# Second gather stage of a graph network: 44 of 782 row gathers replaced by one-hot products on TensorE

## The reference

```python
# layer 0: messages scaled per edge, 32 relations made of 8 basis matrices
W_rel = einsum('rb,bdf->rdf', w_comp, weight)
agg = segment_sum(h[src] * norm, etype * n_nodes + dst)
x = layernorm(x + relu(einsum('rnd,rdf->nf', agg, W_rel) + h_bias + h @ loop_weight))
# layer 1: edge features, two batch norms over all edges, mean per target node
e = (h[dst] - h[src]) @ theta_w.T + h[src] @ phi_w.T
e = relu(bn(e, bn0_g, bn0_b))
e = relu(bn(e @ fc1_w.T, bn1_g, bn1_b))
x = layernorm(x + relu(segment_sum(e, dst) / max(cnt, 1) + h))
```

## Time and profile before

| | |
|---|---|
| median of three runs | 2591.09 us |
| span of the profiled execution | 2589.5 us |
| TensorE busy in the span | 1883.2 us (73%), 10210 products |
| VectorE busy | 1326.0 us (51%) |
| ScalarE busy | 618.8 us (24%) |
| GpSimd busy | 1604.8 us (62%) |
| gathers of the second stage (L698) | 782, 943 ns each, 737.7 us busy |

### The profile page before, as it was taken

The page is one execution under the profiler, slowest core; times in us unless marked ns, Lnnn a source line. Parts: engine busy times, 40 slices in busy tenths (PEclk is TensorE's granted clock), DMA queues, the critical chain, the costliest instruction groups (busy, mean ns, idle before and its releaser), DMA issues. The chain is left out here.

```text
span 2589.5 us, 40626 instructions
## 1 busy us (share of the span) xinstructions
PE 1883.2 (73%) x10210; PEld 1458.7 (56%) x10211; DVE 1326.0 (51%) x2996; ACT 618.8 (24%) x1004; POOL 1604.8 (62%) x1759
## 2 busy tenths in 40 slices
PE   4776767677777778666666666666666899999997
PEld 3766766666666667433333333333333443999996
DVE  5444343434434435654444444444444688677776
ACT  3211111111111113311111111111111675344444
POOL 6777777777777772777777777777777100950002
PEclk9988888888888889655555555555555899999999
DMA  4222222222222222534333433343334795344442
GB/s 105 74 64 72 72 64 72 69 67 71 64 72 72 64 59 68 174 123 125 114 113 117 128 114 113 113 131 114 114 113 131 272 305 175 104 152 147 150 146 83
DMA packets 124081, 291.20 MB, mean 112 GB/s; under 512 B 34957, under 2 KB 77506, under 8 KB 106224
## 3 DMA queue, kind: packets, MB, share of 16 engines
q1 hardware_dynamic: 65856, 136.12, 16.3%
q0 software_dynamic: 50048, 102.50, 15.2%
q10 hardware_dynamic: 8112, 51.91, 5.4%
HBM read 227.22 MB, written 63.18 MB: 112 GB/s over the span
## 5 line engine op out<-in xcount | busy, mean ns | idle before, releaser
L698 POOL DMA_INDIRECT G<-btab,srcT x782 | 737.7, 943 | 282.2 <-issue 180.1
L683 POOL DMA_INDIRECT G<-in_x,srcT x782 | 744.7, 952 | 246.3 <-issue 180.1
L781 PE MATMUL PS<-BIG,G 128*128 128x192 f32 x1564 | 355.8, 380 | 261.2 <-PEq L56 259.1
L907 PE MATMUL PS<-ident,G 128*128 128x128 f32 x784 | 213.4, 428 | 353.5 <-PEq L56 353.5
L781 PEld LDWEIGHTS PS<-BIG,G 128*128 128x128 f32 x1564 | 298.0, 220 | 292.3 <-issue 291.6
L907 PEld LDWEIGHTS PS<-ident,G 128*128 128x128 f32 x784 | 140.2, 217 | 446.5 <-issue 446.5
L1039 ACT ACTIVATE BIG<-PS 128x768 f32<-128x768 f32 x196 | 158.5, 809 | 785.9 <-ACTq L56 785.9
L1474 DVE TENSOR_SCALAR ohT<-PS,node_col 80x512 bf16<-80x512 f32 x196 | 146.2, 746 | 360.6 <-DVEq L56 360.4
L792 PE MATMUL PS<-BIG 128*128 128x192 f32 (+1 forms) x1584 | 328.7, 369 | 0.5 <-PEq L56 0.5
L792 PEld LDWEIGHTS PS<-BIG 128*128 128x128 f32 x1584 | 318.3, 227 | 0.6 <-issue 0.6
L1094 ACT ACTIVATE BIG<-PS 128x512 f32<-128x512 f32 x196 | 117.0, 597 | 841.9 <-ACTq L56 841.9
(11 more groups left out here) (183 smaller groups left out, 1841.6 us busy)
## 6 DMA issues: line engine op xcount, KB each, us to landing
BIG<-spill SPq DMA_DIRECT2D x90, 1024.0 KB, 4.9
spill<-BIG ACTq DMA_DIRECT2D x49, 1024.0 KB
G<-in_x,srcT POOLq DMA_INDIRECT x782, 2.5
G<-btab,srcT POOLq DMA_INDIRECT x782
typ_i<-in_edge_type SPq DMA_DIRECT2D x97, 128.0 KB
BIG<-atab SPq DMA_DIRECT2D x196, 60.0 KB
atab<-BIG SPq DMA_DIRECT2D x12, 384.0 KB, 2.8
xn<-in_x SPq DMA_DIRECT2D x48, 64.0 KB
```

What stands on the lines that cost most here:

```text
L683: nc.gpsimd.indirect_dma_start(out=G[0:n, g % 2, t, :], out_offset=None, in_=x, in_offset=bass.IndirectOffsetOnAxis(ap=srcT[0:n, TPG * g + ...
L698: nc.gpsimd.indirect_dma_start(out=G[0:n, g % 2, t, :], out_offset=None, in_=btab[:, :], in_offset=bass.IndirectOffsetOnAxis(ap=srcT[0:n, ...
L781: mm = pe.matmul(PS[:, 2 * c + q // 2, (q % 2) * ZW:(q % 2 + 1) * ZW], G[:, h, TPC * k + q, :], soh[:, p, TPC * c + q, :, :].rearrange("p ...
L907: pe.matmul(PS[:, 2 + k, q * TILE:(q + 1) * TILE], G[:, h, TPC * k + q, :], ident[:, :], start=(q == 0), stop=False, is_transpose=True, sk ...
```

## The change

In the pairs 2 to 23 the last two tiles of the pair (256 edges) are no longer gathered. The table `btab` is put into SBUF once, as three bf16 parts that add up to the f32 value, 49 windows of 128 nodes: eight units of four windows in the space of `ACC`, which is free in this stage, the rest in `tab_more`. This is done beside the first 13 chunks (`unit_high_part`, `unit_mid_part` on ScalarE, `unit_rest_part`, `unit_low_part` on VectorE, `load_unit` on SyncE).

For a pair's 256 edges, SyncE loads two rows, 64 times the low seven bits of each source and its high bits (`load_pick`). TensorE spreads them over the partitions in one product (`spread_picks`), and ScalarE adds -64 times the partition's number (`code_picks`); the code at partition p is then equal to w exactly when the source is node p of window w. VectorE compares the code with each w (`pick_hots`), which gives a one-hot matrix of 128 x 256 in bf16 for each window; code and result are single rows of 256 (`PICK_ROW, PICK_COLS, PICK_STEP = 1, 256, 256`). TensorE multiplies each window's three parts by it (`pick_rows_of`) and adds the 147 products up in PSUM bank 4. The 49 windows are done in seven batches of seven: one each beside chunks 1 to 5 of the pair, two beside chunk 6 (`picked_batches`), with room for two batches of one-hots. In chunk 7 TensorE transposes two tiles in place of four, and the lookups go in halves into the chunk's bank and bank 4. The chunks' banks are now two in place of four. GpSimd's last memset of `ACC` waits until the last picked chunk is copied.

```diff
+    PICK = 2 * TILE
+    PICK_Q = TPC - 2
+    FIRST_PICK = 2
+    PICK_ROW, PICK_COLS, PICK_STEP = 1, 256, 256
+    BATCH = 7
+    ACC_UNITS = 8
...
+        def picking(g, h, use):
+            return not last(g, NG) and not (isinstance(use, int) and use < FIRST_PICK)
+        def picks(g, h, use, k):
+            return picking(g, h, use) and h == 1 and k == CPG - 1
+        def picked_batches(g, h, use, k):
+            if not picking(g, h, use):
+                return ()
+            at_c = CPG * h + k
+            return {1: (0,), 2: (1,), 3: (2,), 4: (3,), 5: (4,), 6: (5, 6)}.get(at_c, ())
...
+            def load_unit(u):
+                n = len(real_windows(u))
+                take(sp, unit_free)
+                sp.dma_start(bst[:, u % 2, 0:n * D].rearrange("p (w d) -> p w d", w=n),
+                             btab[u * WPB * TNODES:(u * WPB + n) * TNODES, :].rearrange("(w p) d -> p w d", p=P)).then_inc(unit_in[u % 2], 16)
+            sp.sem_inc(unit_free, 2)
+            load_unit(0)
+            load_unit(1)
...
-                    for q in real_tiles(g, k):
+                    for q in swept_tiles(g, g % 2, g // 2, k):
...
+            pool.wait_ge(tab_read, ODD - FIRST_PICK)
             nc.gpsimd.memset(ACC[:, :], 0.0).then_inc(acc_zero, 1)
...
+            def spread_picks():
+                take(pe, pick_rows_in, 16)
+                pe.matmul(pick_spread, onesb[0:2, :], pick_rows[0:2, :], start=True, stop=True,
+                          skip_group_check=True).then_inc(pick_spread_done, 1)
+            def pick_rows_of(b):
+                if b == 0:
+                    take(pe, pick_copied)
+                take(pe, pick_oh_ready)
+                for w in range(BATCH * b, BATCH * (b + 1)):
+                    for a in range(3):
+                        mm = pe.matmul(picked, table_part(w, a), pick_oh[:, BATCH * (b % 2) + w % BATCH, 0:PICK],
+                                       start=(w == 0 and a == 0), stop=False, skip_group_check=True)
+                mm.then_inc(pick_oh_free, 1)
...
-                        for q in range(TPC):
-                            pe.matmul(PS[:, 2 + k, q * TILE:(q + 1) * TILE], G[:, h, TPC * k + q, :], ident[:, :],
+                        for q in (range(PICK_Q) if picks(g, h, use, k) else range(TPC)):
+                            pe.matmul(PS[:, 2 + k % 2, q * TILE:(q + 1) * TILE], G[:, h, TPC * k + q, :], ident[:, :],
                                       start=(q == 0), stop=False, is_transpose=True, skip_group_check=True)
...
-            act.sem_inc(e_free, CPG)
+            act.sem_inc(e_free, 2)
+            def unit_high_part(u):
+                if u >= 1:
+                    act.wait_ge(tab_ready, u)
+                act.wait_ge(unit_in[u % 2], 16 * (units_before[u % 2] + u // 2 + 1))
...
+                act.activation(table_unit(u)[:, :, 0, :], of, ACT.Copy)
+                act.activation(unit_bank(u), of, ACT.Copy).then_inc(unit_high, 1)
+            def unit_mid_part(u):
+                take(act, unit_rest)
+                act.sem_inc(unit_free, 1)
+                act.activation(table_unit(u)[:, :, 1, :], unit_bank(u), ACT.Copy).then_inc(unit_mid, 1)
...
+            def unit_rest_part(u):
+                take(dve, unit_high)
+                dve.tensor_tensor(unit_bank(u), unit_bank(u), table_unit(u)[:, :, 0, :], ALU.subtract).then_inc(unit_rest, 1)
+            def unit_low_part(u):
+                take(dve, unit_mid)
+                dve.tensor_tensor(table_unit(u)[:, :, 2, :], unit_bank(u), table_unit(u)[:, :, 1, :], ALU.subtract).then_inc(tab_ready, 1)
...
+            def pick_hots(b):
...
+                    take(dve, pick_oh_free)
+                for w in range(BATCH * b, BATCH * (b + 1)):
+                    ins = dve.tensor_scalar(pick_oh[:, BATCH * (b % 2) + w % BATCH, :].rearrange("p (r c) -> p r c", r=PICK_ROW),
+                                            pick_code[:, :, 0:PICK_COLS], float(w), None, ALU.is_equal)
+                ins.then_inc(pick_oh_ready, 1)
...
                         if nxt:
                             look_up(nxt[3])
                             count_hots(nxt[0], nxt[3])
+                        for b in picked_batches(g, h, use, k):
+                            pick_hots(b)
```

More of the change, by code:

```diff
@@ L170, in gnn_kernel @@
         floor_row = sb("floor_row", [P, D])
[L171 to L172 removed]
+        diag, diag_t = (typ_i[:, k * D:(k + 1) * D].bitcast(F32) for k in range(2))
+        tab_more = sb("tab_more", [P, (NW - ACC_UNITS * WPB) * 3 * D], BF16)
         loop_s = sb("loop_s", [P, D])
@@ L626, in one @@
                             further_windows(sp, reach, further)
-                by_pairs(sp, NG, one)
+                        u = unit_of(g, k)
+                        if u is not None and u >= 2:
+                            load_unit(u)
+                        if isinstance(g, int) and (g, k) == (2 * FIRST_PICK - 1, 0):
+                            store_picks()
+                by_pairs(sp, NG, one, head=FIRST_PICK)
             sp.wait_ge(widest_c_known, 1)
@@ L897, in spread_dst, with lookup_targets @@
                           start=True, stop=True).then_inc(d_ready, 1)
+            def spread_picks():
[11 more added lines that the diff above has]
+                mm.then_inc(pick_oh_free, 1)
+            def lookup_targets(g, h, use, k):
+                if picks(g, h, use, k):
+                    return (PS[:, 2 + k % 2, 0:PICK], slice(0, PICK)), (picked, slice(PICK, CHUNK))
+                return ((PS[:, 2 + k % 2, :], slice(0, CHUNK)),)
             def edge_features(wide_chunks):
@@ L935, in one @@
                             spread_dst(*nxt)
-                by_pairs(pe, NG, one)
+                        if isinstance(g, int) and (g, k) == (2 * FIRST_PICK - 1, CPG - 1):
+                            pe.wait_ge(tab_ready, NBU)
+                        if picking(g, h, use) and h == 0 and k == 0:
+                            spread_picks()
+                        for b in picked_batches(g, h, use, k):
+                            pick_rows_of(b)
+                by_pairs(pe, NG, one, head=FIRST_PICK)
             pe.wait_ge(widest_c_known, 1)
@@ L1093, in store_e @@
                     act.sem_inc(aw_free, 1)
-                    act.activation(stage[:, stage_of(g, h), k * CHUNK:(k + 1) * CHUNK], PS[:, 2 + k, :],
-                                   ACT.Copy).then_inc(act_self, 1)
-                    take(act, act_self)
+                    to = stage[:, stage_of(g, h), k * CHUNK:(k + 1) * CHUNK]
+                    if picks(g, h, use, k):
+                        act.activation(to.rearrange("p (a n) -> p a n", a=2), PS[:, 2 + k % 2:4 + k % 2, 0:PICK], ACT.Copy).then_inc(act_self, 1)
+                        take(act, act_self)
+                        act.sem_inc(pick_copied, 1)
+                        act.sem_inc(tab_read, 1)
+                    else:
+                        act.activation(to, PS[:, 2 + k % 2, :], ACT.Copy).then_inc(act_self, 1)
+                        take(act, act_self)
                     act.sem_inc(e_free, 1)
                     act.sem_inc(e_copied, 1)
+                    if u is not None:
+                        unit_mid_part(u)
+                    if picking(g, h, use) and h == 0 and k == 0:
+                        code_picks()
                 act.sem_inc(dig_free, 1)
                 act.dma_start(spill[bass.ds(g, 1), :, :].rearrange("o p n -> (o p) n"), stage[:, stage_of(g, h), :]).then_inc(stored[h], 16)
-            by_pairs(act, NG, store_e, tail=HELD // 2)
+            by_pairs(act, NG, store_e, head=FIRST_PICK, tail=HELD // 2)
             take(act, e_measured, 2)
@@ L1509, in one @@
                             count_hots(nxt[0], nxt[3])
+                        u = unit_of(g, k)
+                        if u is not None:
+                            unit_rest_part(u)
+                        if isinstance(g, int) and (g, k) == (1, 1):
+                            split_picks()
+                        for b in picked_batches(g, h, use, k):
+                            pick_hots(b)
                         if wide_chunks:
@@ L1528, in one @@
                         pair_moments()
-                by_pairs(dve, NG, one, tail=HELD // 2)
+                by_pairs(dve, NG, one, head=FIRST_PICK, tail=HELD // 2)
             look_up(0)
```

97 lines of the change are left out of this document (87 added, 10 removed).

## The result

The changed kernel takes 2624.05 us in the median (four runs, 2620.37 to 2629.57), the kernel before 2591.99 (four runs): a ratio of 1.0125, interval [1.0110, 1.0139]. The forecast was 2546, and its range ended at 2616. The profiled run of the changed kernel took 2622.85 us, with a span of 2621.0.

A forecast was written before the change was run, and what follows sets the result against it. GpSimd's gathers, one every 1.248 us, were taken to bound the second gather stage. The sum: 2591.1 - 54.9 (gathers dropped) + 8 (trains) + 2 (head) = 2546 us, range 2532 to 2616.

The forecast's parts named there:

- I take 0.05 us, the middle of what GpSimd lost there: 154 x 0.05 = 8 us: Second gather stage: each of 154 one-hot trains beside GpSimd's gathers costs them 0.05 us, adding 8 us.
- Break-even: Loss per one-hot train at which the change gains nothing: 54.9 / 154 = 0.36 us.
- ends of 0 and 0.88 us: Bounds on a train's cost to gathers: 0 if its gaps suffice, 0.88 us if GpSimd is shut out throughout.
- trains shut GpSimd out until they end: First rival, second gather stage: 0.88 us lost per train, 135 us in all, time 2673; chance 0.21.
- its cheaper step: First rival with VectorE at four columns a cycle: train 1.0 us, loss 0.48 us each, time 2612.
- the geometry: Where a 1.4 us train begins in a gather's 1.25 us period sets that gather's or the next one's delay, mean 0.88.
- My 0.20: VectorE's assumed step per 256-column one-hot, 0.20 us, making 9.8 us a pair.
- disagrees with a lock that outlasts it: Reading of the earlier trace: one VectorE instruction blocks a gather, but the lock does not last beyond that instruction.
- GpSimd's 54.9 us: Second gather stage: 44 gathers dropped at 1.248 us each save 54.9 us while GpSimd stays slowest.
- TensorE's clock: Second gather stage: picking products wake the clock, 33.4 us a pair within 37.4; low-clock rival 2940 us, chance 0.05.
- the pace: Rival: VectorE or TensorE becomes slowest in the paired stage, pairs 38.5 to 40.5 us, time 2561 to 2605; chance 0.14.
- The head: First 13 chunks, table split and loading: GpSimd may stall for a buffer, 0 to 5 us, taken as 2.

## Why the prediction was wrong

**The step that failed** is "I take 0.05 us, the middle of what GpSimd lost there: 154 x 0.05 = 8 us". Measured: 84 us, or 0.55 for each of 154 batches. In the trace, 110 trains of seven lose 0.53 us each on the mean and 22 trains of fourteen 1.12. Break-even was worked out at 0.36, so this one term turned the sign. With it the sum reads 2591.1 - 54.9 + 84 = 2620, and 2 us more behind the last gather, 2622; the profiled run took 2622.85.

**Why it was chosen.** Two rows spoke. The earlier trace rows showed a single instruction holding a gather until its end; the 13 instructions in the earlier trace rows showed a train beside which GpSimd got its turn, and I preferred it because it was a train. But those 13 work on f32, 128 columns, with numbers from columns, beside ordinary GpSimd instructions; the one-hots are bf16, 256 columns, with a constant, beside gathers. The 0.05 us was also what one GpSimd instruction lost there, not what the train cost: in the trace four stand beside the 13 (878, 833, 837 and 833 ns in place of 791) and lose 0.22 us together. Form decides: a constant turned into a column took the loss from 84 to 52 us, one row turned into three took it to 0. The nearest row by shape of the sequence was not the nearest by kind of instruction, and ends of 0 and 0.88 us with break-even at 0.36 called for a wide range and no strong middle.

**The rival that came true** is the first, "trains shut GpSimd out until they end", at its cheaper step: 0.48 us a train, 2612. It lay 12 us low. 8 of these are the loss of a train of seven, 0.53 us in place of 0.48; a part of that is that the geometry let a train catch a gather only in its first 0.46 us, while in the trace those that begin up to 0.54 us into it still do. That 44 of the batches stand in pairs, as 22 trains of fourteen, adds only 1 us, as these lose little more than twice as much. The rest, about 2 us, is what the median of the runs lies above this sum. The Trainium skill (VectorE: DVE Perf Modes, the perf-mode tier table) gave this step: its four columns a cycle made an estimate of 0.14 us, and the trace agrees with 0.135. My 0.20 was wrong, and with it this rival lay at 2673. Of the Trainium skill's other rule (SBUF — State Buffer, Who interferes with whom: the loser is fully blocked) I wrote that the trace "disagrees with a lock that outlasts it". In these trains the hold does outlast a single instruction, up to the end of all seven (1.02 us) or fourteen (1.97).

**GpSimd's 54.9 us** were right. With three rows of 87 and no stretch the kernel takes 2594.77 - 2540.03 = 54.7 us less than the one before, and its last gather starts at 1958.0, where it was 2012.9 and "near 1960" was forecast.

**TensorE's clock** rose as argued: 0.86 in the stage, and 5 again where 20 of 21 picking products are left out. Also as argued, the first batch of a pair, behind the chunks that have none, is mostly slow (0.20 us a product on the mean of 22 pairs) and the next is at the higher level (0.11). A pair of 30 gathers takes 30 x 931.20 / 679 = 41.1 us, and TensorE is busy for 764.05 / 931.20 of it, 33.8 us, where 33.4 were worked out. One batch reads in the timeline:
```profile
1559.56 2.45 PE L987 MATMUL PS<-BIG,ACC 128*128 128x256 bf16 x21
1563.35 0.63 PE L1005 MATMUL PS<-ident,G 128*128 128x128 f32 x4 [1.34 <-PEq L36]
```
After 21 products, 0.117 us each, TensorE still waits 1.34 us for the next gathers. No cost, as forecast.

**VectorE** is not the pace in the changed kernel, 570.26 of 931.20 us; with a wait after each one-hot it is. **The head** cost nothing: no gather but the first, which waits for the table, stood idle ahead for more than 0.3 us. That 2.2 us stand behind the last gather instead makes up for the 2 us taken here only by chance.

## What to carry to other kernels

Before you hide VectorE's work beside gathers that GpSimd issues, look for one row in which an instruction of that very form (type, constant or column, one row or several) meets a gather, and price a back-to-back train by where the train ends, not by its single instructions. If the gathers set the pace, a slower form of the instruction that leaves them alone is the faster kernel: three rows in place of one cost VectorE 0.06 us a step and gave 84 us back. When a remedy is a wait, count what it adds on the engine that waits: one or two in seven helped, six in seven moved the bound. To move the pieces apart without a wait gave back less, 35 us; there look also at what stands directly ahead of a piece.

## What the runs showed of the hardware

- A train of one-hots that follow at 0.135 us holds a gather from 944 up to 2743 ns, and the gather ends 0.82 or 0.12 us behind the train. Of the 122 gathers of over 1 us none ends ahead of its train; a wait in between lets them go (948 ns with one after each). A train that begins 0.57 us or later into a gather leaves that gather alone, with one exception at 0.63.
- Directly behind the lookup's one-hot, three such instructions hold a gather that began 0.34 us before them (1.64 us in place of 0.94).
- The same comparison over rows of 3 x 86 or 3 x 87 at a pitch of 88 takes 0.194 to 0.198 us a step and stretches no gather beyond 961 ns. The Trainium skill (VectorE: DVE Perf Modes, Mode 2×_2P) says that an instruction can use both read ports only where the outermost dimensions of source and destination are even, or equal. In the trace's operands the source here has three rows and the destination is one run of 258 or 261, so the two are neither both even nor equal, and the longer step agrees; no run tried other shapes.
- With the number read from a column the step was 0.196 us, and the gathers still averaged 1013 ns.
